# Window attention's value product: one head at a time, or all heads at once and the right one picked afterwards

## What is computed

```python
h = _layernorm(win, ln1_g, ln1_b)                    # windows of 7 x 7 = 49 positions
q, k, v = (h @ wq), (h @ wk), (h @ wv)               # each .reshape(-1, 49, 3, 8): 3 heads of 8
attn = einsum('nqhd,nkhd->nhqk', q, k) / sqrt(8) + mask
attn = softmax(attn, axis=-1)
out = einsum('nhqk,nkhd->nqhd', attn, v).reshape(-1, 49, 24)
out = out @ wo + bo
```

## Time and profile before

| | |
|---|---|
| median of 3 runs | 4035.52 us (4033.6 to 4039.21) |
| the profiled execution, its own time | 4016.56 us |
| its span | 4014.8 us |
| TensorE matmul busy | 3420.1 us, 85% of the span |
| VectorE busy | 1756.6 us, 44% |
| ScalarE busy | 1812.1 us, 45% |
| GpSimd busy | 231.9 us, 6% |
| granted TensorE clock, mean | 0.942 |

### The profile page before, as it was taken

How to read it: one execution, slowest core, us unless ns; L and a number is a source line. 1 busy time by engine, 2 the same in 40 slices (tenths; PEclk the granted TensorE clock), 3 DMA queues, 4 the chain that set the end, 5 groups by cost and what they waited for, 6 DMA issues and landing times.

```text
span 4014.8 us, 132263 instructions
## 1 busy us (share of the span) xinstructions
PE 3420.1 (85%) x59692; PEld 2370.5 (59%) x59692; DVE 1756.6 (44%) x2866; ACT 1812.1 (45%) x3411; POOL 231.9 (6%) x489
## 2 busy tenths in 40 slices
PE   3988889888898888987989879898789887898987
PEld 1737656467455584565854747547566484664855
DVE  3533455344543436434463344533445334453344
ACT  1453444533455434544345444453444534435344
POOL 3500000000000000000000000000000000000000
PEclk8989999899999999999999989999998998999999
DMA  4111000110010100101001010010100100001000
GB/s 126 40 44 28 2 14 6 41 28 3 14 29 18 28 3 14 45 2 28 3 15 44 3 27 3 15 45 3 27 2 15 44 16 14 2 16 28 22 9 14
DMA packets 24173, 88.38 MB, mean 22 GB/s; under 512 B 17843, under 2 KB 18211, under 8 KB 19643
## 3 DMA queue, kind: packets, MB, share of 16 engines
q1 hardware_dynamic: 22339, 74.72, 7.7%
q0 software_dynamic: 1280, 5.21, 0.5%
HBM read 63.86 MB, written 14.84 MB: 20 GB/s over the span
## 4 chain that ended last, share of the span: by engine, by line
PE 76%; ACT 10%; DVE 6%; issue 4%; SPq 3%; DMA 1%; ACTq 0%; DVEq 0%
PE ps L1007 76%; ACT lv L614 3%; ACT rs L619 3%; DVE area_ty L840 2%; SPq L426 1%; DVE xs L977 1%; DVE area_ty L928 1%; ACT area_ty L706 1%; ACT area_ty L700 1%; DVE area_hz L861 1%; DMA area_ty<-area_hz 1%; ACT sq L606 1%; DVE area_ty L973 0%; ACT area_ty L749 0%; DVE area_hz L877 0%
## 5 line engine op out<-in xcount | busy, mean ns | idle before, releaser
L840 DVE TENSOR_TENSOR area_ty<-ps,rs 128x448 f32<-128x448 f32 (+2 forms) x416 | 285.2, 686 | 546.9 <-ACT rs L619 546.9
L725 ACT ACTIVATE area_ty<-ps 120x448 f32<-120x448 f32 (+1 forms) x448 | 243.5, 543 | 439.7 <-PE ps L1007 439.7
L1007 PE MATMUL ps<-area_hz 32*64 32x147 f32 (+2 forms) x7180 | 371.4, 293 | 82.6 <-DVE area_hz L861 31.6
L949 DVE COPY area_ty<-ps 120x448 f32<-120x448 f32 (+1 forms) x432 | 270.0, 625 | 388.1 <-PE ps L1007 388.1
L1007 PE MATMUL ps<-area_ty,area_hz 113*64 113x49 f32 (+1 forms) x10240 | 397.0, 251 | 32.5 <-DMA area_ty<-area_hz 29.9
L1007 PE MATMUL ps<-sq,keep_sb 128*128 128x448 f32 (+1 forms) x832 | 393.6, 575 | 29.9 <-ACT sq L606 21.4
L725 ACT ACTIVATE area_hz<-ps 112x384 f32<-112x384 f32 (+2 forms) x384 | 190.9, 497 | 489.1 <-PE ps L1007 489.1
L1007 PEld LDWEIGHTS ps<-area_hz 32*64 32x64 f32 (+2 forms) x7180 | 293.3, 158 | 192.9 <-issue 165.9
L1007 PEld LDWEIGHTS ps<-area_ty,area_hz 113*64 113x64 f32 (+1 forms) x10240 | 335.0, 136 | 110.8 <-issue 110.5
L1007 PE MATMUL ps<-keep_sb,area_hz 112*56 112x56 f32 (+1 forms) x12288 | 365.7, 222 | 11.3 <-ACT area_hz L725 11.2
L1007 PEld LDWEIGHTS ps<-keep_sb,area_hz 112*56 112x56 f32 (+1 forms) x12288 | 362.1, 133 | 13.6 <-ACT area_hz L725 13.4
(11 more groups left out here) (108 smaller groups left out, 4006.4 us busy)
## 6 DMA issues: line engine op xcount, KB each, us to landing
area_hz<-f_all SPq DMA_DIRECT2D x16, 2541.0 KB
xw<-x_in SPq DMA_DIRECT2D x8, 1568.0 KB, 6.5
y_out<-xs SPq DMA_DIRECT2D x32, 294.0 KB
f_all<-piece POOLq DMA_DIRECT2D x16, 317.6 KB, 3.5
area_ty<-area_hz SPq DMA_DIRECT2D x256, 4.6 KB
area_hz<-raw_in SPq DMA_DIRECT2D x1, 2894.0 KB, 9.2
g_sb<-g_in SPq DMA_DIRECT2D x2, 1396.5 KB
g_sb<-g_in SPq DMA_DIRECT2D x1, 1470.0 KB
```

Of the source, the lines that this page charges most:

```text
L725: act.activation(dst, src, ACT.Relu if st in (ST_H, ST_F2) else ACT.Copy).then_inc(sc_kept, 1)
L840: ve.tensor_tensor(o, a, b, ALU.mult, **kw).then_inc(normed, 1)
L949: ins = ve.tensor_copy(dst, src)
L1007: return pe.matmul(o, a, b, start=start, stop=stop)
```

## The change

Each value product now takes all three heads at once: the moving side is the 147 columns of a window (3 heads x 49 positions), the stationary side holds all 24 channels of the values in one block, without zeros between heads. There are 4 products a step in place of 12. The result has, for every head's probabilities, the values of all heads; it fills 294 columns of bank 4 in a step, so ScalarE copies it to `o3` after every step, and TensorE's next value product waits for that copy.

Of the 3 x 49 columns of a window, each channel needs those of its own head. `pick` is a 128 x 3 table of zeros and ones, by partition and head. After the last step of a row ScalarE writes head 0's columns times `pick[:, 0]` to `osb`, and VectorE adds head 1's times `pick[:, 1]` and then head 2's times `pick[:, 2]`, each waiting for the one before. The spread product waits for the last of them (`picked`). The table is made once by five small VectorE instructions. The old copy of a row into `osb` is gone, the zeroing covers a `ring` of a third of the size, and the values and ones are written to it in longer runs.

```diff
--- before.py
+++ after.py
@@ -250,6 +250,9 @@
         wq = sb("wq", [128, 128])
         wk = sb("wk", [128, 128])
         wv = sb("wv", [128, 2, 2 * C])
+        pick = sb("pick", [128, NH])
+        pick4 = sb("pick4", [128, 4, QI])
+        pick1 = sb("pick1", [128, 2, 4])
         ident = sb("ident", [128, 128])
         spread = sb("spread", [128, 128])
         w1 = sb("w1", [128, HID])
@@ -303,13 +306,15 @@
         lns, at = part(area_y, at, TW)
         rec, at = part(area_y, at, TW)
         assert at <= NTOK
-        ring = area_z.rearrange("p (b u n) -> p b u n", b=2, n=NH * PADL)
-
-        def value_blocks(b, jj):
-
-            base = ring[64 * jj:64 * jj + L, b, :, 32 * jj:32 * jj + 1]
-            return bass.AP(base.tensor, base.offset,
-                           [*base.ap[0:1], [NH * PADL, 2 * NW], [PADL + DH, NH], [1, DH]])
+        ring, at = part(area_z, 0, 2, 2 * NW, PADL)
+        o3, at = part(area_z, at, 2, NW, NH * L)
+        assert at <= 64 * PAIR
+
+        def head_out(b, h):
+            return o3[:, b, :, L * h:L * h + L]
+
+        def head_sum(b):
+            return osb[:, b, :].rearrange("p (w n) -> p w n", n=L)
 
         hid, _ = part(area_y, 0, 4, 2, TW)
 
@@ -350,8 +355,11 @@
         scored, maxed = sem("scores_made"), sem("row_max")
         max_turned, max_kept, max_rows = sem("max_turned"), sem("turned_max_kept"), sem("max_rows_written")
         cross, exped, weighed = sem("turned_scores_made"), sem("probs_ready"), sem("values_weighed")
-        out_kept, sum_spread, sum_logged, sum_inverted = (
-            sem("pair_out_kept"), sem("sums_spread"), sem("sum_logged"), sem("sum_inverted"))
+        out_kept, first_picked, second_picked, picked = (
+            sem("step_out_kept"), sem("first_head_picked"), sem("second_head_picked"),
+            sem("heads_picked"))
+        sum_spread, sum_logged, sum_inverted = (
+            sem("sums_spread"), sem("sum_logged"), sem("sum_inverted"))
         out_normed, projected, attended = sem("out_normed"), sem("projected"), sem("attention_added")
         ring_ready, pads_ready = sem("value_ring_zeroed"), sem("mixer_pads_zeroed")
         up_made, geglu, down_made, mlp_added, reordered = (
@@ -470,16 +478,14 @@
             def zero_ring():
 
                 gp.memset(qk[:, :, :, L:PADL], 0.0)
-                gp.memset(area_z, 0.0).then_inc(pads_ready, 1)
+                gp.memset(ring, 0.0).then_inc(pads_ready, 1)
 
             def ones_in_ring():
 
                 gp.sem_inc(passed_gp, 1)
                 for jj in range(2):
                     r = slice(64 * jj, 64 * jj + L)
-                    for h, c in ((0, 24), (1, 25), (2, 26), (0, 27)):
-                        o = PADL * h + RW * jj + c
-                        ins = gp.memset(ring[r, :, :, o:o + 1], 1.0)
+                    ins = gp.memset(ring[r, :, :, RW * jj + C:RW * jj + C + 4], 1.0)
                 ins.then_inc(ring_ready, 1)
 
             gp.wait_ge(su_ve, N_SETUP_VE)
@@ -629,18 +635,27 @@
             def window_attention(q):
                 for n in range(-8, STEPS + 4):
                     t, dw = n // 4, n % 4
+                    k = n - 2
+                    if 0 <= k < STEPS:
+                        u = k // 4
+                        act.wait_ge(weighed, q * STEPS + k + 1)
+                        if k % 4 == 0 and u >= 2:
+                            act.wait_ge(picked, q * NW + u - 1)
+                        act.activation(o3[:, u % 2, 2 * (k % 4):2 * (k % 4) + 2, :],
+                                       ps[:, 4, 0:6 * L].rearrange("p (w n) -> p w n", w=2), ACT.Copy
+                                       ).then_inc(out_kept, 1)
+                        if k % 4 == 3:
+                            act.wait_ge(out_kept, q * STEPS + k + 1)
+                            if u >= 2:
+                                act.wait_ge(out_normed, q * NW + u - 1)
+                            act.activation(head_sum(u % 2), head_out(u % 2, 0), ACT.Copy,
+                                           scale=pick[:, 0:1]).then_inc(first_picked, 1)
                     if 0 <= n < STEPS:
                         act.wait_ge(cross, q * STEPS + n + 1)
                         if n >= 2:
                             act.wait_ge(weighed, q * STEPS + n - 1)
                         act.activation(pt[0:SIDE, n % 2, :, :], ps[0:SIDE, 2:4, 0:6 * L], ACT.Exp
                                        ).then_inc(exped, 1)
-                    if dw == 0 and 0 <= t - 1 < NW:
-                        act.wait_ge(weighed, q * STEPS + 4 * t)
-                        if t - 1 >= 2:
-                            act.wait_ge(out_normed, q * NW + t - 2)
-                        act.activation(osb[:, (t - 1) % 2, :], ps[:, 4, 0:TW], ACT.Copy
-                                       ).then_inc(out_kept, 1)
                     if dw == 0 and t + 2 < NW:
                         u = t + 2
                         act.wait_ge(k_made, q * NW + u + 1)
@@ -757,6 +772,7 @@
 
             act.preload_act_table_set("natural_log_exp_and_others")
             norm(0, LN_FIRST)
+            act.wait_ge(su_ve, N_SETUP_VE + 5)
             for q in range(nq):
                 window_attention(q)
                 mlp(q)
@@ -869,6 +885,13 @@
                                                 ALU.add, ALU.add).then_inc(attended, 1)
                     if dw == 0 and 0 <= t - 3 < NW:
                         scale_windows(q, LN_WIN2, t - 3)
+                    if dw == 0 and 0 <= t - 1 < NW:
+                        b = (t - 1) % 2
+                        for h, ready, done in ((1, first_picked, second_picked),
+                                               (2, second_picked, picked)):
+                            ve.wait_ge(ready, q * NW + t)
+                            ve.scalar_tensor_tensor(head_sum(b), head_out(b, h), pick[:, h:h + 1], head_sum(b),
+                                                    ALU.mult, ALU.add).then_inc(done, 1)
                     if dw == 1 and t + 2 < NW:
                         u = t + 2
                         ve.wait_ge(k_kept, q * NW + u + 1)
@@ -888,9 +911,9 @@
                             ve.wait_ge(weighed, q * STEPS + 4 * u - 4)
                         for jj in range(2):
                             ins = ve.tensor_copy(
-                                value_blocks(u % 2, jj),
+                                ring[64 * jj:64 * jj + L, u % 2, :, RW * jj:RW * jj + C],
                                 ps[64 * jj:64 * jj + L, 7, 0:NW * 2 * C].rearrange(
-                                    "p (u h d) -> p u h d", h=NH, d=DH))
+                                    "p (u c) -> p u c", c=C))
                         ins.then_inc(v_kept, 1)
                     if dw == 3 and t + 2 < NW:
                         u = t + 2
@@ -991,6 +1014,15 @@
 
             for i in range(NW):
                 scale_windows(0, LN_FIRST, i)
+            ve.wait_ge(pads_ready, 3)
+            su(ve.tensor_reduce(pick4[:, :, :], ident[:, :].rearrange("p (j h d) -> p h j d", j=QI, d=DH),
+                                AX.X, ALU.add))
+            su(ve.tensor_reduce(pick1[:, 0, :], pick4[:, :, :], AX.X, ALU.add))
+            su(ve.tensor_reduce(pick1[:, 1, :],
+                                spread[:, :].rearrange("p (j h d) -> p h d j", j=QI, d=DH)[:, :, 0],
+                                AX.X, ALU.add))
+            su(ve.tensor_tensor(pick[:, :], pick1[:, 0, 0:NH], pick1[:, 1, 0:NH], ALU.add))
+            su(ve.tensor_tensor(pick[:, 0:1], pick[:, 0:1], pick1[:, 1, NH:NH + 1], ALU.add))
             for q in range(nq):
                 window_attention(q)
                 scale_windows(q, LN_WIN2, NW - 1)
@@ -1091,16 +1123,16 @@
                         pe.wait_ge(exped, q * STEPS + k + 1)
                         if k % 4 == 0:
                             pe.wait_ge(v_kept, q * NW + u + 1)
-                            if u >= 1:
-                                pe.wait_ge(out_kept, q * NW + u)
+                        if k >= 1:
+                            pe.wait_ge(out_kept, q * STEPS + k)
+                        pe.sem_inc(passed_pe, 1)
                         for i in range(2):
                             w = 2 * (k % 4) + i
-                            for h in range(NH):
-                                for g in range(2):
-                                    o = NH * L * i + L * h
-                                    ins = mm(ps[PADL * g:PADL * g + PADL, 4, L * w:L * w + L],
-                                             ring[0:SIDE, u % 2, 2 * w + g, PADL * h:PADL * h + PADL],
-                                             pt[0:SIDE, k % 2, g, o:o + L], start=h == 0, stop=h == NH - 1)
+                            o = NH * L * i
+                            for g in range(2):
+                                ins = mm(ps[PADL * g:PADL * g + PADL, 4, o:o + NH * L],
+                                         ring[0:SIDE, u % 2, 2 * w + g, :],
```

(3 more changed lines are left out.)

## The result

The changed kernel takes 4093.27 us (median of 4 runs, 4091.06 to 4102.17); the kernel before, run beside it, 4034.56 us (median of 4, 4021.08 to 4039.21). The ratio is 1.0155 with an interval of 1.0127 to 1.0184: slower by 59 us, where +94 was forecast (4130, range 4095 to 4172). The profiled execution of after took 4102.17 us, with a span of 4100.5 at a mean granted clock of 0.934; the one of before 4016.56 us, 4014.8 and 0.942. Between the two profiled executions the difference is therefore 86 us, not 59: the profiled run of before is 18 us under its own median, and that of after 9 us above. What lies outside the attention, and moves between runs of one and the same kernel, is the subject of the last experiments.

A forecast was written before the change was run, and what follows sets the result against it. TensorE's blocks were taken to bound the attention stage's steady rows. Shorter value products less new stalls gave +11.2 us a stage, +90 for eight, +4 for the clock: 4035.5 + 94 = 4130, range 4095 to 4172.

The forecast's parts named there:

- The steady row: One row of windows in the attention stage: 13.83 us now, 14.94 after, from 0.76 saved and three stalls added.
- The case's own range: Ends for value block, pick and copy lengths: +9.2 to +14.5 us a stage, total 4108 to 4155.
- The value block: TensorE's value product in each step: 0.65 us in place of 0.84, 0.19 saved a step, 49 us over the kernel.
- The rival that the rounds don't get cheaper: Value product: load and stream in series, block stays at 0.86, +16 us a stage, 4165; chance 0.06.
- Stall 1, the spread: TensorE's spread product waits for the picks behind ScalarE's k and q copies: 1.08 us a row.
- Stall 2, the masked k: The k mask, queued behind the picks on VectorE, comes late for TensorE: 0.23 us a row.
- Stall 3, behind the norm: At a row's first step ScalarE's copy stands behind the norm's Ln and Exp, delaying the value product: 0.56 us.
- The other rows: Non-steady rows of a stage: first -0.2 us, second +0.55, third +0.9, fourth to sixth +1.1 each, seventh +1.35.
- The last row: Last row and drain, where no scores, k or q cover the waits: stalls sum to 9.0 us, net +5.3 a stage.
- The clock rival: TensorE's clock falls to half in the rows too: up to +178 us more, 4275 with part under the stalls; chance 0.06.
- Setup: Smaller first zeroing starts the first norm 3.5 us sooner, five small VectorE instructions follow; neither counts, the maxima's DMA covers them.
- the change in a stage's length should carry over: Step from profiled execution to median, 19 us above it: 4035.5 + 94 = 4130.

The follow-up runs named there:

- the last experiments: The kernel before timed again unchanged, 4035.52 us; SyncE's second table load started some 8 us later in three kernels, 4002.52, 4100.12 and 4012.08 us.
- wide_only: The changed kernel's 147-column products with the waits and one copy a row of the kernel before, no picks: 4041.58 us median, quicker runs' ratio 0.9836.
- after_table: The changed kernel with SyncE's second table load waiting for the stage behind the mixer, some 8 us later: 4100.12 us, ratio 1.0161.
- early_norm: The changed kernel with only the copy of each row's third step moved ahead of the norm's Ln and Exp: 4148.6 us, ratio 1.0279.
- run 70: Not a run's label but part of "profiled run 70 us": early_norm's profiled run has 70 us more than the changed kernel's outside the attention stages.

## Why the prediction came out as it did

**Right: the sign, the place and the mechanism.** The steady row was worked out at 14.94 and is 14.77, with the stops in the three places named and released by the instructions named. The stages came out at +97.7 us against +90. (The case's own range should begin at 4109 and not at 4108: 4035.5 and eight times 9.2.)

**The value block** was put at 0.65 and is 0.66. The rival that the rounds don't get cheaper fell, and with it the rule of the Trainium skill ("TensorE: Matmul & The Clock Gate", The mechanism) that a weight load overlaps a running matmul only when the row groups differ: here they never differ, and the block would have stayed near 0.86 by the forecast's reckoning. The same section also lets a load run ahead into the background weight buffer; no run here tells what hides the loads. What the step lacked is that *wide_only* gains 0.54 a row and not 0.76: where no gap stands ahead of the wide value product, the k and q products behind it take 0.2 more. In after a gap stands there, and they don't.

**Stall 1, the spread,** 1.08 forecast, is 1.13 from the end of TensorE's work (1.05 in the profile's row). The terms erred against each other. The copy took 0.405 where 0.42 was put; but the first pick 0.627 and the two later ones 0.63 each (1.29 from the start of one to the end of the other) where 0.53 and 0.57 were put. Rows of before with one or two full operands, L664 and L909, were taken for instructions that have a column per partition as a further operand; L868, the other end that the forecast named (0.62), is of that form. What made up for it is that ScalarE starts its copy 0.1 us before the last instruction's end in the trace, where 0.05 after it was counted.

**Stall 2, the masked k,** 0.23 forecast, is 0.10, by the same overlap. **Stall 3, behind the norm,** 0.56 forecast, is 0.46: ScalarE's copy and the Exp after it overlap by 0.1 (677.91 + 0.40 against 678.20).

**The other rows** from one Exp to the next: the third 14.38 (13.81 before), the fourth to sixth 14.71 to 14.8 (13.83), the seventh 12.21 (11.11), that is +0.57, +0.9 and +1.1 where +0.9, +1.1 and +1.35 were put. **The last row** is +6.8 where +5.3 was put (21.3 for 14.5). Its timeline on TensorE:

```profile
711.08 0.72 PE L1039 MATMUL ps<-area_ty,area_hz 113*64 113x147 f32 x8 [0.90 <-issue]
713.59 0.72 PE L1039 MATMUL ps<-area_ty,area_hz 113*64 113x147 f32 x8 [0.28 <-issue]
717.39 0.72 PE L1039 MATMUL ps<-area_ty,area_hz 113*64 113x147 f32 x8 [1.56 <-issue]
720.61 1.68 PE L1039 MATMUL ps<-area_ty,spread 128*128 128x392 f32 x2 [2.49 <-DVE area_ty L893]
724.09 1.68 PE L1039 MATMUL ps<-area_ty,keep_sb 128*128 128x392 f32 x2 [0.50 <-DVE area_ty L932]
```

The stalls are those laid out (1.7 and 2.4 forecast, 1.56 and 2.49 read). But the last products run at half clock: 1.68 for two records of 392 columns that take 0.93 at full. The clock fell inside the last row, at 718.9, behind gaps of 0.90, 0.28 and 1.56 us (before: at 704.7, 4 us behind the stage's end); the prediction had put this term behind the drain, at 0.5 us a stage. It is about 1.5, inside it: 0.6 for the spread and 0.7 for the product at 724.09, each counted to the next start, and a part of the last.

**The clock in the rows** stayed at 1.00 in the steady row, as forecast, with one exception, the first group. There three of VectorE's picks took 1.85, 1.50 and 1.43 us in place of 0.63 (at 130.2, 146.2 and 163.2), each while GpSimd ran its addition L517 beside it. The spread waited 1.9 us behind the last two, and the clock then fell to half for 3.4 us each time (at 148.9 and 166.0). This is a part of what makes that stage 123.8 us long. The clock rival was real in one group of eight, and a pick slowed by GpSimd was in no list.

**Setup** made no difference: the first turned scores start at 100.61 (100.41 before). The five small instructions took 275 to 159 ns.

**Wrong: that only the stage changes.** The sum of +94 is near the change's own price, 97.6 measured without the stops, with the stages put 8 us too low and 4 us added for the clock. What was timed is +59, because before loses some 31 us to stops in its mixer and after none. The step that failed is "the change in a stage's length should carry over" to the median. Of the 39 us between 97.6 and 59 the stops are 31; the other 7 are the distance between the medians of *after_table* and after, inside the scatter of both. That after has no stop is luck as far as is known: *early_norm*, with the same instructions on TensorE, has eight, which cost its profiled run 70 us; with them the change would have measured some +130 (an estimate: 59 + 70). The stops stood in the trace of before, in stages that the change doesn't touch, and the forecast left them out.

## What to carry over

When an engine has spare time, what an added instruction costs is its place in the queue: the same copy and picks cost 1.25 us a row behind k and q and nothing ahead of them, as long as the row has work to cover them; work out what stands before them and where the cover ends, the drain above all. A gain taken from the product's own block (0.76 a row) can shrink (to 0.54) in the products behind it. And look for idle time with "issue" as its releaser next to a large transfer also in the stages that a change doesn't touch: here a load started 8 us later brought 31 us, and the stop's coming and going moved the timing by a third of the change and more. The list of DMA packets by queue, instruction fetches among them, says what such an idle time waited for.

## What the runs showed of the hardware

- TensorE can stop for want of instructions beside a large load, without any semaphore between them: 4.3 to 6.1 us, 4 to 7 us behind the issue of 2541 KB. It went on 1.5 to 1.7 us after the next 16 KB packet of the instruction queue had landed. The granted clock then falls (*early_norm*: 0.57 over 12 us and 0.85 over the next 64, where after has 0.87 and 0.92), in all some 7 to 10 us for each stop. Busy time around the stop of before, 6.5 of 12 us:

```profile
372.00:384.00 12.00, 6.52 (x38) 2.10 (x38) 1.35 (x3) 0.54 (x1) 0.00 (x0) 0.57 0.56 121
```

- Whether it comes isn't settled by the program on TensorE: kernels with the same loads had it in none, half or all of their groups, after and *early_norm* with the same TensorE instructions in none and in all, and one kernel was at 3973 us or at 4043 us with nothing changed.
- Four rounds of 147 columns on 113 rows, two records each, took 0.66 us with their weight loads hidden.
- A multiply-add of 392 elements with a column per partition took 0.627 us on VectorE and a copy scaled by such a column 0.627 on ScalarE; the product of two tiles of before (L909) took 0.57 and an activation without the column (L664) 0.53. Beside GpSimd's addition L517 the multiply-add took 1.43 to 1.85 us.
- Behind the stalls of the last row TensorE came to half clock inside it, and the two records of a product of 392 columns went from 0.93 to 1.68 us.
